# A six-stage decoder kernel: four stages written out without engine loops, and the normalised input read where it lies

## The reference

```
layer 0: a0  attention in 4 branches x 16 heads, 256 tokens: weights = softplus of the scores,
             capped, times a sigmoid, small ones set to zero, then normalised
         x0  linear attention on a context: q = x Wq, k = ctx Wk, v = ctx Wv; focused features
         f0  "switch" attention: 16 heads, 8 experts of which 2 are chosen per token and head
layer 1: a1  8 heads of 128 against 1024 keys of a context
         x1  16 heads of 64 against the context, with a mask
         f1  mixture of experts: a shared and a routed hidden layer (silu gate), 8 experts in
             2 groups, 2 chosen per token
```

## Time and profile before

| | |
|---|---|
| three runs | 3120.69, 3126.18, 3129.67 us, median 3126.18 |
| span of the profiled execution | 3124.2 us (first to last instruction; the page gives no other time of it) |
| busy | PE 2720.5 (87%), DVE 1999.9 (64%), ACT 1747.3 (56%), POOL 792.9 (25%) |
| mean granted TensorE clock | 0.928 |
| DMA | 57.76 MB, 6.0% of 16 engines; instruction queues 91 and 58 packets |

### The profile page before, as it was taken

The page is one execution under the profiler, slowest core; times in us unless marked ns, Lnnn a source line. Parts: engine busy times, 40 slices in busy tenths (PEclk is TensorE's granted clock), DMA queues, the critical chain, the costliest instruction groups (busy, mean ns, idle before and its releaser), DMA issues. The chain is left out here.

```text
span 3124.2 us, 50399 instructions
## 1 busy us (share of the span) xinstructions
PE 2720.5 (87%) x17384; PEld 2036.1 (65%) x17384; DVE 1999.9 (64%) x4360; ACT 1747.3 (56%) x3237; POOL 792.9 (25%) x887
## 2 busy tenths in 40 slices
PE   6778888888876689999979999999979999949998
PEld 3344444444435556777658888888867777748887
DVE  4788778778865756655646666666666556545444
ACT  3888887878874444444435555555555555542221
POOL 1122212222210134444432111111005566610000
PEclk8789889988878899999999999999989999969999
DMA  3000000000001111111010000000010000020000
GB/s 102 4 4 4 0 3 3 0 3 3 1 1 52 68 46 24 24 29 42 21 34 13 6 6 3 6 1 1 1 66 8 8 5 5 2 95 7 3 7 30
DMA packets 88677, 57.76 MB, mean 18 GB/s; under 512 B 55120, under 2 KB 78544, under 8 KB 88016
## 3 DMA queue, kind: packets, MB, share of 16 engines
q1 hardware_dynamic: 88528, 55.80, 6.0%
HBM read 39.00 MB, written 8.39 MB: 15 GB/s over the span
## 5 line engine op out<-in xcount | busy, mean ns | idle before, releaser
L672 DVE SCALAR_TENSOR_TENSOR a_w<-a_w,a_sinks 128x384 f32<-128x384 f32 x512 | 332.8, 715 | 32.0 <-ACT a_w L507 32.0
L2033 POOL TENSOR_SCALAR x_weights<-x_weights,x_sums 128x256 f32<-128x256 f32 x256 | 231.8, 924 | 275.0 <-DVE x_sums L2092 275.0
L1125 POOL TENSOR_SCALAR f_weights<-f_weights,f_sums 128x256 f32<-128x256 f32 x256 | 232.0, 924 | 272.9 <-DVE f_sums L1355 272.9
L486 ACT ACTIVATE a_e<-psum 128x1024 f32<-128x1024 f32 x192 | 195.4, 1018 | 155.7 <-PE psum L345 114.7
L1283 ACT ACTIVATE f_weights<-psum,f_negmax 128x256 f32<-128x256 f32 x256 | 117.7, 472 | 215.2 <-DVE f_negmax L1349 215.2
L1619 ACT ACTIVATE a_turned_w_hi<-psum 128x512 fp32r<-128x512 f32 x256 | 139.1, 596 | 152.0 <-PE psum L1529 151.9
L687 DVE SCALAR_TENSOR_TENSOR a_w<-a_e,psum 128x512 f32<-128x512 f32 x256 | 162.8, 677 | 92.8 <-ACT a_e L488 88.0
L342 PE MATMUL psum<-a_qT,a_kT_half 32*128 32x512 f32 x512 | 165.8, 727 | 60.4 <-DVE a_w L687 49.3
L488 ACT ACTIVATE a_e<-a_e 128x1024 f32<-128x1024 f32 x192 | 202.9, 1057 | 6.1
L2003 ACT ACTIVATE x_weights<-x_masked_s,x_negmax 128x256 f32<-128x256 f32 x256 | 127.0, 497 | 138.6 <-DVE x_negmax L2084 138.6
L1735 DVE TENSOR_REDUCE a_negmax<-psum 128x1 f32<-128x1024 f32 x128 | 156.7, 1224 | 65.7 <-PE psum L123 61.5
(11 more groups left out here) (361 smaller groups left out, 7725.5 us busy)
## 6 DMA issues: line engine op xcount, KB each, us to landing
f_xnT<-all_xnT_all SPq DMA_DIRECT2D x16, 256.0 KB, 2.3
f_pv_rows<-f_pv SPq DMA_DIRECT2D x8, 512.0 KB, 3.1
f_pv_groups<-f_pv_rows SPq DMA_DIRECT2D x8, 512.0 KB
f_w<-in_f_w SPq DMA_DIRECT2D x2, 2048.0 KB, 10.0
all_x_all<-in_x SPq DMA_DIRECT2D x1, 2048.0 KB, 8.4
a_xnT<-all_xnT_all SPq DMA_DIRECT2D x8, 256.0 KB, 2.3
x_xnT<-all_xnT_all SPq DMA_DIRECT2D x8, 256.0 KB, 2.3
x_ctxT<-in_x_ctxT SPq DMA_DIRECT2D x8, 256.0 KB, 2.7
```

What stands on the lines that cost most here:

```text
L486: act.activation(e[:, x, :], psS[x], ACT.Exp).then_inc(exp_done, 1)
L672: ins = dve.scalar_tensor_tensor(part, part, sinks[:, col:col + 1], part, ALU.is_ge, ALU.mult)
L1125: ins = pool.tensor_scalar(w, w, sums[:, k, h, t:t + 1], None, ALU.mult)
L2033: ins = pool.tensor_scalar(w, w, sums[:, k, h, t:t + 1], None, ALU.mult)
```

## The change

`over_batches` becomes a Python loop, and f1's four loops and SP's loops in a0, x0 and f0 too: every batch number is a constant, and no register is computed. The tile `xnT`, its semaphore, its waits and its copies go from a0, x0, f0 and f1; the products and roundings read `xnT_all[:, b]`. In f1 ScalarE's rounding waits for `projected` instead of the copy. `each_batch` of x1 is dropped for `over_batches`, which is now the same.

```diff
 def over_batches(eng, body):
-    body(-1, False, True, False)
-    body(0, True, True, False)
-    with eng.Fori(0, B - 2) as i:
-        body(i + 1, True, True, True)
-    body(B - 1, True, False, True)
-    body(B, False, False, True)
+    for b in range(-1, B + 1):
+        body(b, 0 <= b < B, b + 1 < B, b >= 1)
...
 # a0
-            with sp.Fori(0, B) as b:
-                sp.wait_ge(v_done, b)
-                sp.dma_start(xnT[:], xnT_all[:, bass.ds(b, 1), :, :]).then_inc(v_x_here, 16)
...
-                        pe.wait_ge(v_x_here, bb * 16 + 16)
-                                ins = pe.matmul(spare[...], xnT[:, c, t * P:(t + 1) * P], wv[:, c, :],
+                                ins = pe.matmul(spare[...], xnT_all[:, bb, c, t * P:(t + 1) * P], wv[:, c, :],
...
 # x0
-            with sp.Fori(0, B) as b:
+            for b in range(B):
                 sp.wait_ge(projected, b * 3)
-                sp.dma_start(xnT[:], xnT_all[:, bass.ds(b, 1), :, :]).then_inc(x_here, 16)
                 sp.dma_start(ctxT[:], a["ctxT"][bass.ds(b * D, D), :].rearrange("(k p) n -> p k n", p=P))\
...
-                pe.wait_ge(x_here, b * 16 + 16)
                 pe.wait_ge(ctx_here, b * 16 + 16)
...
 # f0
-            sp.dma_start(xnT[:], xnT_all[:, 0]).then_inc(x_here, 16)
...
                 sp.wait_ge(pv_taken, b * TT + TT)
-                if more:
-                    sp.dma_start(xnT[:], xnT_all[:, bass.ds(b + 1, 1), :, :]).then_inc(x_here, 16)
                 sp.dma_start(pv_rows[rows].rearrange("(t p) e d -> p t (e d)", p=P), pv[:]).then_inc(stored, 16)
...
-            body(0, True)
-            with sp.Fori(0, B - 2) as i:
-                body(i + 1, True)
-            body(B - 1, False)
+            for b in range(B):
+                body(b)
...
-                    pe.wait_ge(x_here, bb * 16 + 16)     (gate and pv)
-                            ins = pe.matmul(here[...], xnT[:, c, t * P:(t + 1) * P], wg[:, c, :],
+                            ins = pe.matmul(here[...], xnT_all[:, bb, c, t * P:(t + 1) * P], wg[:, c, :],
...
 # f1
-            with sp.Fori(0, B) as b:
-                sp.wait_ge(low, b * (1 + NHID))
-                sp.dma_start(xnT[:], xnT_all[:, bass.ds(b, 1), :, :]).then_inc(x_here, 16)
...
-            with pe.Fori(0, B) as b:
-                pe.wait_ge(x_here, b * 16 + 16)
-                pe.wait_ge(shifted, b)
+            for b in range(B):
+                wait(pe, shifted, b)
...
-            with act.Fori(0, B) as b:
-                act.wait_ge(x_here, b * 16 + 16)
-                act.activation(xnT_hi[:], xnT[:], ACT.Copy).then_inc(high, 1)
+            for b in range(B):
+                wait(act, projected, b * NHID)
+                act.activation(xnT_hi[:], xnT_all[:, b], ACT.Copy).then_inc(high, 1)
...
-            with dve.Fori(0, B) as b:
+            for b in range(B):
                 dve.wait_ge(high, x_split(b))
-                dve.tensor_tensor(xnT_lo[:], xnT[:], xnT_hi[:].bitcast(F32), ALU.subtract).then_inc(low, 1)
+                dve.tensor_tensor(xnT_lo[:], xnT_all[:, b], xnT_hi[:].bitcast(F32), ALU.subtract).then_inc(low, 1)
```

More of the change, by code:

```diff
@@ L765, in project @@
             def project(b):
-                pe.wait_ge(x_here, b * 16 + 16)
                 pe.wait_ge(ctx_here, b * 16 + 16)
                 wait(pe, features_raw, b)
-                for n, (src, weights) in enumerate(((ctxT, wk), (xnT, wq), (ctxT, wv))):
+                for n, (src, weights) in enumerate(((ctxT, wk), (xnT_all[:, b], wq), (ctxT, wv))):
                     if n == 2:
@@ L1057, in switch_attention @@
         uT = s.sb("uT", [P, KO, T])
-        x_here, gated, gates_taken, sig_ready, own_gates, chosen, pv_ready, pv_taken = (
-            s.sem(n) for n in ("x_here", "gated", "gates_taken", "sig_ready", "own_gates", "chosen", "pv_ready", "pv_taken"))
+        gated, gates_taken, sig_ready, own_gates, chosen, pv_ready, pv_taken = (
+            s.sem(n) for n in ("gated", "gates_taken", "sig_ready", "own_gates", "chosen", "pv_ready", "pv_taken"))
         stored, blocks_here, picks_here, blank = (s.sem(n) for n in ("stored", "blocks_here", "picks_here", "blank"))
@@ L1076, in _, with body @@
         def _(sp):
-            sp.dma_start(xnT[:], xnT_all[:, 0]).then_inc(x_here, 16)
-            def body(b, more):
+            def body(b):
                 rows = bass.ds(b * T, T)
@@ L1152, in beside_pair @@
                 elif kind == "gate":
-                    pe.wait_ge(x_here, bb * 16 + 16)
                     for t in range(TT):
                         for c in range(CC):
-                            ins = pe.matmul(here[:, t * D:(t + 1) * D], xnT[:, c, t * P:(t + 1) * P], wg[:, c, :],
+                            ins = pe.matmul(here[:, t * D:(t + 1) * D], xnT_all[:, bb, c, t * P:(t + 1) * P], wg[:, c, :],
                                             start=(c == 0), stop=(c == CC - 1))
@@ L1159, in beside_pair @@
                 elif kind == "pv":
-                    pe.wait_ge(x_here, bb * 16 + 16)
                     for c in range(CC):
-                        ins = pe.matmul(here, xnT[:, c, i * P:(i + 1) * P], wv[:, c, :], start=(c == 0), stop=(c == CC - 1))
+                        ins = pe.matmul(here, xnT_all[:, bb, c, i * P:(i + 1) * P], wv[:, c, :], start=(c == 0), stop=(c == CC - 1))
                     ins.then_inc(pv_ready, 1)
@@ L1805 @@
                6: [("qk", 3, AHEAD), ("qk", 4, AHEAD)], 7: [("qk", 5, AHEAD)]}
-def each_batch(eng, body):
-    for b in range(-1, B + 1):
-        body(b, 0 <= b < B, b + 1 < B, b >= 1)
 def cross_attention1(nc, norm, x_all, xnT_all, ident, psum, a):
@@ L1961, in body @@
                         ins.then_inc(summed, 1)
-            each_batch(pe, body)
+            over_batches(pe, body)
         @block.scalar
@@ L2018, in body @@
                                        ACT.Copy).then_inc(turned_taken, 1)
-            each_batch(act, body)
+            over_batches(act, body)
         @block.gpsimd
@@ L2040, in _ @@
             pool.wait_ge(loaded, 16 * len(loads))
-            each_batch(pool, body)
+            over_batches(pool, body)
         @block.vector
@@ L2123, in body @@
                            .then_inc(oT_ready, 1)
-            each_batch(dve, body)
+            over_batches(dve, body)
 HID, NE, NGR = 512, 8, 2
@@ L2162, in experts @@
         acc = s.sb("acc", [P, TT, D])
-        loaded, x_here, projected, silu_done, hidden_taken = (
-            s.sem(n) for n in ("loaded", "x_here", "projected", "silu_done", "hidden_taken"))
+        loaded, projected, silu_done, hidden_taken = (
+            s.sem(n) for n in ("loaded", "projected", "silu_done", "hidden_taken"))
         gates_ready, shifted, exp_done, own = s.sem("gates_ready"), s.sem("shifted"), s.sem("exp_done"), s.sem("own")
```

15 lines of the change are left out of this document (5 added, 10 removed).

## The result

| kernel | time, us (median) | ratio to before, 95% interval | profiled span |
|---|---|---|---|
| before, run beside it | 3124.24 | | 3124.2 |
| changed | 3101.1 (3099.5 to 3108.8) | 0.9923 [0.9911, 0.9935] | 3097.7 |

What follows compares the result with a forecast made beforehand. Stages run one after another, with TensorE the largest engine; its waits for copies and loop register work were to go: f0 -7.5, x0 -2.4, a0 -2.1, f1 0, together -12.0 us, from 3126.18 to 3114.2 us, range 3103 to 3126.

Steps and rivals of the forecast that it cites:

- f0, the copies: f0: earlier loads end TensorE's waits for `mix_blocks` in six looped batches, -4.6 us; batch 0 loses a copy's issue, -0.5.
- f0, the start: f0's first gate product no longer waits for the first copy to land and starts with the block: -2.4 us.
- x0 (-2.4): x0: context loads go ahead without the copy, -1.4 us in batches 0 and 1; six later batches give -1.0.
- can give back that 0.17 and no more: x0 from batch 2 on: an earlier transfer saves only the 0.17 us idle ahead of the projection, six batches, -1.0 us.
- a0 (-2.1): a0: the loop's register work costs 0.35 us in each of six looped batches, which goes: -2.1 us.
- with the same rate in the other five: a0: 0.13 us between batches 6 and 7 in three steps, extended over eight: 0.35 us a batch.
- f1 (0): f1: neither the copy nor the loop's turn is paid for, so no gain: 0 us, bounds -0.8 and +10.
- rival B: TensorE's clock in f0 and f1: more batches fall to the low level, +12.8 us, cancelling the gain, 3127; chance 0.06.
- A: Only copies count; in f0 another wait replaces that for `mix_blocks`, a0 gives nothing: -4.3 us, 3122; chance 0.11.
- B in reverse: No f0 or f1 batch at the low clock, -9.4 us, with a0's register cost at its upper bound: 3100 to 3105; chance 0.11.
- C: Written-out code in a0, f0 and f1 fetches 62 more instruction blocks, each stopping TensorE: +19 us, 3145; chance 0.08.
- D: Each of 26 loop turns stops its engine for a code fetch of 2.4 us; without loops, 3064; chance 0.02.

Runs made afterwards that it cites:

- Experiment 4: The kernel before with only f0's first copy removed, batch 0 reading the normalised input in place; all loops and other copies stay: 3124.56 us, 0.9997.
- experiment 8: The kernel before with f1 alone changed: 3123.78 us, 0.9983; also the changed kernel with a0 alone put back as before: 3109.05 us, 0.9934.

## Why the prediction missed by half

- **f0, the copies (-4.6 right, -0.5 in batch 0 not seen).** 62.2 us against 62.3. Batch 0 takes 61.05 us, 61.08 before. Batch 1 was to lose 1.8 and still varies, 62.2 to 63.1 in the changed kernel, so the six together give 4.2 to 5.0.
- **f0, the start (-2.4): mechanism right, size wrong.** The forecast moved the product's start by the landing it waited for, and left the eight products at the duration of the earlier trace rows. They were slow because of the pause ahead of them. The step failed at "the product can start with the block": the products start 2.2 us earlier and run at full clock, and the first exponential comes 5.3 us earlier. The stated upper bound, "the whole idle time", -3.1, was no bound, since what a pause does to the clock is not in the pause. Experiment 4 shows it alone, and also that the stage needn't keep it.
- **x0 (-2.4): mechanism right, mis-sized.** The step "can give back that 0.17 and no more" failed. It measured 0.4 a batch in five, 2.2 in all, where six times 0.17 was forecast: the printed idle time behind a pipelined product was taken as the whole wait. The start gave 1.0 and the wait ahead of batch 1 0.7, where 0.7 twice was forecast. Batch 1 itself is 1.6 us shorter, and the sum has no term for that: TensorE is busy 10.88 us in it before, at a mean clock of 0.75, and 9.46 now, at 0.84. The tail took 0.9 back. -4.7 in all.
- **a0 (-2.1): wrong.** The step that failed is "with the same rate in the other five": the 0.13 us between batches 6 and 7 was an offset, not a cost of every step. The batch takes 109.2 with loops and 109.0 to 109.5 without. What the stage gained, 3.2 us in its tail, is the clock; one written-out profile of seven kept the long tail. That the first pair of profiles gave -2.6, near the forecast -2.1, is luck. Why the writing out shifts the slow stretches there was not found.
- **f1 (0): wrong, and the largest miss.** The turn "0.02 us behind the store" of the earlier trace rows was read as costing nothing. But written out, the split starts 0.08 us before the store's printed end, so the turn costs 0.10 us on VectorE, and 0.16 on TensorE; with the 0.50 us pause that follows growing to 0.66 the period at full clock really is the same, 39.08 and 39.05. But with the pause of 1.06 us the clock falls behind half of the turns and with 0.90 behind none: -5.3 us by experiment 8. The step that failed is "I take 0", which left the clock out of the turn. I had the earlier trace rows in hand, priced the fall at 1.5 us, and treated it as something that happens to a kernel (rival B) and not as something a shorter pause ends.
- **The sum now**, by averages over the profiles in which a stage's code is as before and those in which it is as changed: a0 -3.0 us, x0 -4.5, f0 -7.5, a1 +0.2, x1 -3.4, f1 -5.7, together -23.9. By the ratios -24.1 and -26.9 were measured. a0 and x1 move by several us between profiles of the same code, so their terms are rough. f0's -7.5 equals the forecast by luck: its start gave -4.1 on average (-5.3 where nothing else delayed it), its batches -5.0, and its tail took 1.7 back (4.2 in the first profile). Why the tail grew wasn't isolated.
- **Rivals.** A falls (f0 kept its waits' gain). B in reverse, fewer low stretches, is what happened in f1, at f0's start and in a0's tail. Its 3100 to 3105 holds the measured 3101.1, in part by chance: one of f0's middle batches is low in the first profile of the changed kernel and two in the second, and the register cost in a0 that it added is nothing. (It also counted four low batches in f1 where its own text has three of six, so -9.4 should be -7.9 and +12.8 should be +11.3.) C falls: 50 more blocks fetched by q8 and 29 by q14, no idle time behind one, batches no longer. D falls: the turns of a0 and f0 cost nothing that shows, and f1's 0.10 us on VectorE.
- **Open.** x1's tail is 65.2 to 66.4 us in three of the five profiles in which TensorE loops in x0 and f0, and 58.7 to 60.4 in the other two and in all nine others. Fourteen profiles can't tell whether the change makes the long one rarer; if it does, x1's -3.4 us belong to the gain. That f1's clock holds because the pause is shorter fits every profile, but it was tried with one length only, 1.12 us, and gave one fall; where the pause lies may matter too.

## What to carry to other kernels

A pause of TensorE has two prices: its length, and the products behind it if the clock falls; so price a copy or a turn that makes TensorE wait a microsecond at both, and read the products behind it in the trace, not only the idle time before. Order an engine's queue so that what others wait for is issued first: swapping two DMA issues, and the waits for them, gave x0's middle batches the same 8.61 us as the removal of the copy (though the total didn't show it, 1.0001). And look at what runs beside a single slow instruction: `COPY` of 2.04 us amid neighbours of 0.69 was visible in the trace of the changed kernel (1.45 in that of before), and moving GpSimd's clears under a normalisation, together with f1's split ahead of its sums, made the version with the lowest ratio, 0.9886 (0.9907 without the moved clears, a difference that is not clear of noise).

## What the hardware did that I had not expected

- TensorE's clock fell to half for 3.4 us behind 15 of 30 pauses of 1.06 to 1.09 us, 1 of 6 of 1.12 us and 0 of 36 of 0.90 us, in f1's middle batches, with the same products around them. Once fallen it costs 1.5 us a batch.
- VectorE's fp32 copy from SBUF to SBUF took 0.43 us alone, 1.4 to 2.2 beside one clear of GpSimd, 5.56 behind the rest of one and the whole of the next, and 6.04 behind some thirteen small ones in a row. Reductions and two-input operations of the same shape beside the same clears kept their 0.69.
- A clear that VectorE's copy slips in front of is itself longer: the second clear took 3.79 us there, and 3.51 elsewhere.
